# Attention and a feed-forward layer on one core: idle PE products at the start, norms spread over the last iterations, and the last down products in four banks

## The reference, cut to what matters

```python
x = x + _layernorm(_L0_attn_ref(_layernorm(x, axis=-1), L0_attn_Wq, L0_attn_Wk, L0_attn_Wv, L0_attn_Wo, ...))
x = x + _layernorm(_L0_ffn_ref(_layernorm(x, axis=-1), L0_ffn_w_gate, L0_ffn_w_up, L0_ffn_w_down), axis=-1)
...
maha = jnp.maximum(qn[..., None] + (E * E)[None] * kn[:, :, None, :] - 2.0 * E[None] * s, 0.0) / V[None]
logits = coef * jnp.log1p(maha / nu[None, :, None, None]) - 0.5 * DH_ * jnp.log(V)[None]
A = jax.nn.softmax(logits, axis=-1)
...
h = jax.nn.silu(gate) * up
return jnp.einsum('bsh,dh->bsd', h, wd)
```

## Time and profile before

| | |
|---|---|
| median of 3 runs | 1877.73 us (1877.56 to 1878.31) |
| profiled execution | 1878.49 us, span 1876.7 us |
| PE busy | 1792.1 us (95%) |
| DVE busy | 1628.9 us (87%) |
| ACT busy | 1580.4 us (84%) |
| POOL busy | 1469.7 us (78%) |
| mean granted clock of PE | 0.988 |

### The profile page before, as it was taken

How to read it: one execution, slowest core, us unless ns; L and a number is a source line. 1 busy time by engine, 2 the same in 40 slices (tenths; PEclk the granted TensorE clock), 3 DMA queues, 4 the chain that set the end, 5 groups by cost and what they waited for, 6 DMA issues and landing times.

```text
span 1876.7 us, 35392 instructions
## 1 busy us (share of the span) xinstructions
PE 1792.1 (95%) x10672; PEld 1476.5 (79%) x10672; DVE 1628.9 (87%) x3848; ACT 1580.4 (84%) x3259; POOL 1469.7 (78%) x1291
## 2 busy tenths in 40 slices
PE   4799999999999999999999999999999999988996
PEld 3577788878888888778888888788888888867886
DVE  7799989988988889888888999888988988895884
ACT  5798889898888889898988888988988888885563
POOL 5677888878888888888888888788888888862663
...
GB/s 187 114 68 46 85 46 68 46 102 46 63 52 90 64 49 44 45 124 46 68 46 99 32 63 52 82 89 49 46 42 91 46 46 46 68 13 12 46 47 44
DMA packets 61085, 117.77 MB, mean 63 GB/s; under 512 B 13489, under 2 KB 42929, under 8 KB 52705
## 3 DMA queue, kind: packets, MB, share of 16 engines
...
q10 hardware_dynamic: 384, 0.00, 0.0%
...
## 4 chain that ended last, share of the span: by engine, by line
PE 72%; DVE 10%; ACT 4%; issue 3%; POOL 1%; DVEq 0%; POOLq 0%; ACTq 0%
PE pa L759 15%; PE py L823 13%; PE ps L799 12%; PE po L834 10%; PE pp L789 8%; PE pp L811 6%; PE pa L770 4%; PE pa L778 2%; DVE lg L1603 2%; DVE stats L1630 1%; DVE rm L1472 1%; DVE acc L1652 1%; DVE tabs L1690 1%; DVE lg L1596 1%; POOL rstd L602 1%
## 5 line engine op out<-in xcount | busy, mean ns | idle before, releaser
L583 POOL TENSOR_TENSOR qk<-rm 64x512 f32<-64x512 f32 x504 | 697.2, 1383 | 93.2 <-PE ps L799 49.1
L593 POOL TENSOR_TENSOR ek<-tabs,kn 128x512 f32<-128x512 f32 (+3 forms) x512 | 463.8, 912 | 126.4 <-DVE lg L1596 99.4
L1603 DVE CUSTOM_DVE_ANT_0 lg<-lg,tabs,ncog 128x512 f32<-128x512 f32 (+3 forms) x512 | 446.7, 890 | 0.0
L759 PE MATMUL pa<-xt,wt 128*128 128x512 f32 x1488 | 421.9, 419 | 4.4 <-DVE rm L1478 2.7
L1472 DVE TENSOR_TENSOR rm<-pa,tabs 128x512 f32<-128x512 f32 x504 | 327.2, 677 | 74.1 <-POOL qk L583 66.1
L799 PE MATMUL ps<-qk 128*128 128x512 f32 (+3 forms) x1024 | 366.5, 442 | 7.8 <-DVE lg L1596 7.6
L823 PE MATMUL py<-pt,vt 128*128 128x128 f32 x2560 | 348.5, 275 | 0.1
L1596 DVE CUSTOM_DVE_ANT_0 lg<-ps,ek,qb 128x512 f32<-128x512 f32 (+3 forms) x512 | 279.3, 546 | 79.3 <-issue 61.1
L823 PEld LDWEIGHTS py<-pt,vt 128*128 128x128 f32 x2560 | 331.7, 192 | 16.2 <-issue 0.3
L759 PEld LDWEIGHTS pa<-xt,wt 128*128 128x128 f32 x1488 | 274.0, 191 | 56.9 <-issue 6.2
L1169 ACT ACTIVATE lg<-lg,qb 128x512 f32<-128x512 f32 (+3 forms) x512 | 273.0, 557 | 14.4 <-DVE lg L1596 10.4
...
## 6 DMA issues: line engine op xcount, KB each, us to landing
...
```

Source lines behind the costliest of these rows:

```text
L583: pool.tensor_tensor(qk[part * DH:(part + 1) * DH, z * HH + hh, :], rm[row, 2 * part, :], rm[row, 2 * part + 1, :], ALU.add if part else A ...
L593: pool.tensor_tensor(ek[:, n % 2, 0:w], tab(par, hh, E2_T, w), kn[:, hh, 0:w], ALU.mult).then_inc(ek_pool, 1)
L759: last = mm(pa[r][:, :], wproj(par, z, kt, a, r * P, (r + 1) * P), xbuf[x][:, kt, b, :], start=(n == 0), stop=(n == 3 * KT - 1))
L1603: dve.tensor_tensor_reduce(lg[:, hh, at(n)], lg[:, hh, at(n)], tab(par, hh, T3_T, w), ncog[:, par, 0, hh:hh + 1], 3e38, ALU.add, ALU.min, ...
```

## The change

*Preparation.* `keep_busy(n)` puts n products of the identity with the token numbers into PE's queue, plain f32, 512 columns, into the two `ps` banks; nobody reads them. Six stand ahead of `x_turn`, one between the two halves of the projections, two ahead of `first_norms_k`.

*Last iterations.* `left` is the number of iterations still to come. The first sequence's `first_norm(0)` moves into the iteration with `left` 3, its residual sum into `left` 2, its `second_norm(0)` into `left` 1, each on DVE between `decay(1,3)` and `distance(1,3)`; the powers on POOL move with them. In the last iteration all four distances of the second head are computed ahead of `add_output`, ACT takes `log(1,3)` with the other logarithms, `f_normal(0)` and `f_high(0)` come ahead of the exponentials, and PE takes `f_transposes(0)` and the first two `gate_up` earlier. The second sequence's norms are spread between `add_output`s.

*Tail.* The last sequence's down products go into four banks, a tile each: parts 0 to 4 of tiles 2 and 3, then of tiles 0 and 1, then part 5 of all. `f_last` is cut in two halves; of the last sequence ACT takes tiles 0 and 1 and DVE tiles 2 and 3 (`last_half`), and there are two stores. `third_norm` waits for two tiles at a time.

```diff
...
@@ -182,2 +182,7 @@
         po = bank("po")
+        last_banks = [py, po, pp[0], pp[1]]
+
+        def down_at(b, j):
+
+            return last_banks[j][:, 0:D] if b == B - 1 else (py, po)[j // 2][:, (j % 2) * D:(j % 2 + 1) * D]
 
...
@@ -530,6 +535,10 @@
                 f_load(b)
-            for b in range(B - 4, B):
+            for b in range(B - 4, B - 1):
                 f_store(b)
-            for s in range(2):
-                sp.wait_ge(f_out[s], 16 * (B // 2))
+            for k, half in enumerate((1, 0)):
+                sp.wait_ge(f_res, B + k)
+                sp.dma_start(out_d[B - 1].rearrange("(j p) n -> p j n", p=P)[:, 2 * half:2 * half + 2, :],
+                             f_outs[(B - 1) % 2][:, 2 * half:2 * half + 2, :]).then_inc(f_out[(B - 1) % 2], 16)
+            sp.wait_ge(f_out[0], 16 * (B // 2))
+            sp.wait_ge(f_out[1], 16 * (B // 2 + 1))
 
@@ -616,4 +625,6 @@
                     low_weights(pool, g, q)
-                if not nxt:
+                if it.left == 2:
                     f_pow(0, 0)
+                if not nxt:
+                    f_pow(1, 0)
                 if nxt:
@@ -627,4 +638,2 @@
                 decay_norm(c, 1, 2, it.par)
-                if not nxt:
-                    f_pow(1, 0)
                 if nxt:
@@ -642,4 +651,2 @@
                     x_rstd(it.own + 3)
-                if not nxt:
-                    f_pow(0, 1)
                 if nxt:
@@ -687,2 +694,3 @@
 
+            f_pow(0, 1)
             f_pow(1, 1)
@@ -889,2 +897,16 @@
 
+            def last_down():
+                b = B - 1
+                for tiles, parts in (((2, 3), range(FT - 1)), ((0, 1), range(FT - 1)), (range(NT), range(FT - 1, FT))):
+                    pe.wait_ge(f_hl, b * FT + parts[-1] + 1)
+                    for j in tiles:
+                        if parts[0] == 0 and j < 2:
+                            pe.wait_ge(f_ev, 2 * (b - 1) + j + 1)
+                        for r in parts:
+                            for a in range(2):
+                                last = mm(last_banks[j][:, 0:D], hpart(b, r, a)[:, j * P:(j + 1) * P], wdt[:, r, :],
+                                          start=(r == 0 and a == 0), stop=(r == FT - 1 and a == 1))
+                        if parts[0] and j % 2:
+                            last.then_inc(f_dn, 1)
+
             PERS = (8, 4, 2, 1)
...
@@ -994,2 +1019,8 @@
 
+            def keep_busy(n):
+
+                for k in range(n):
+                    mm(ps[k % 2][:, :], ident[:, :], tokens, start=True, stop=True)
+
+            keep_busy(6)
             x_turn(c0, 0, 0)
@@ -999,2 +1030,3 @@
             project(c0, 0, 0, 0, 0, 0, 0, 1)
+            keep_busy(1)
             pe.wait_ge(w_lo, 2 * KT)
@@ -1004,2 +1036,3 @@
             x_turn(c0, 1, 1)
+            keep_busy(2)
             first_norms_k()
...
@@ -1054,4 +1085,3 @@
                 gate_up(b, 5)
-            down(B - 1, 0)
-            down(B - 1, 1)
+            last_down()
 
@@ -1222,3 +1252,3 @@
 
-            def f_last(b):
+            def f_last(b, half):
                 act.wait_ge(f_move[2], b + 1)
@@ -1227,7 +1257,6 @@
                 q = 4 + b % 2
-                for j in range(NT):
-                    last = act.activation(f_tmp[:, j, :], (py, po)[j // 2][:, (j % 2) * D:(j % 2 + 1) * D], ACT.Identity,
+                for j in (2 * half, 2 * half + 1):
+                    last = act.activation(f_tmp[:, j, :], down_at(b, j), ACT.Identity,
                                           bias=f_shift[:, 6 + b % 2, j:j + 1], scale=f_rstd[:, q, j:j + 1])
-                    if j % 2 == 1:
-                        last.then_inc(f_ev, 1)
+                last.then_inc(f_ev, 1)
 
...
@@ -1387,2 +1419,4 @@
                 silu(b, 4)
+                if b == B - 1:
+                    f_last(b - 1, 0)
                 hidden_high(b, 4)
@@ -1390,4 +1424,6 @@
                 hidden_high(b, 5)
-                f_last(b - 1)
-            f_last(B - 1)
+                if b < B - 1:
+                    f_last(b - 1, 0)
+                f_last(b - 1, 1)
+            f_last(B - 1, 0)
 
@@ -1646,3 +1682,3 @@
 
-            def residual(b):
+            def residual_sum(b):
 
@@ -1653,2 +1689,4 @@
                 last.then_inc(f_sum, 1)
+
+            def second_norm(b):
                 dve.wait_ge(f_sum, b + 1)
@@ -1656,2 +1694,6 @@
 
+            def residual(b):
+                residual_sum(b)
+                second_norm(b)
+
             def second_move(b):
@@ -1660,4 +1702,7 @@
             def third_norm(b):
-                dve.wait_ge(f_dn, 2 * b + 2)
-                f_stat(2, b, lambda j: (py, po)[j // 2][:, (j % 2) * D:(j % 2 + 1) * D], EPS_LN / SCALE ** 2)
+                def source(j):
+                    if j % 2 == 0:
+                        dve.wait_ge(f_dn, 2 * b + j // 2 + 1)
+                    return down_at(b, j)
+                f_stat(2, b, source, EPS_LN / SCALE ** 2)
 
@@ -1678,2 +1723,20 @@
 
+            def last_half():
+                b = B - 1
+                dve.wait_ge(f_out[b % 2], (b // 2) * 16)
+                dve.wait_ge(f_move[2], b + 1)
+                for j in (2, 3):
+                    last = stt(f_outs[b % 2][:, j, :], down_at(b, j), f_rstd[:, 4 + b % 2, j:j + 1], acc[:, b, j, :],
+                               ALU.mult, ALU.add)
+                last.then_inc(f_sum, 1)
+                dve.wait_ge(f_sum, B + 1)
+                for j in (2, 3):
+                    last = ts(f_outs[b % 2][:, j, :], f_outs[b % 2][:, j, :], f_shift[:, 6 + b % 2, j:j + 1], None, ALU.add)
+                last.then_inc(f_res, 1)
+
+            def last_sum():
+                b = B - 1
+                dve.wait_ge(f_ev, 2 * b + 1)
+                tt(f_outs[b % 2][:, 0:2, :], f_tmp[:, 0:2, :], acc[:, b, 0:2, :], ALU.add).then_inc(f_res, 1)
+
             def split_low(b):
@@ -1712,4 +1775,3 @@
                 if not nxt:
-                    dve.wait_ge(acc_dve, 4 * (B * G - B + 1) + 4)
-                    first_norm(0)
+                    second_move(0)
                 if nxt:
@@ -1737,4 +1799,2 @@
                 logits(c, 0, 3, it.par)
-                if not nxt:
-                    residual(0)
                 decay(c, 1, 2, it.par)
@@ -1752,2 +1812,5 @@
                 distance(c, 1, 2, it.slot)
+                if not nxt:
+                    decay(c, 1, 3, it.par)
+                    distance(c, 1, 3, it.slot)
                 if old:
@@ -1759,5 +1822,6 @@
                     inverse(cp, 1)
-                if not nxt:
-                    second_move(0)
                 logits(c, 1, 1, it.par)
+                if not nxt:
+                    logits(c, 1, 2, it.par)
+                    split_low(0)
                 if nxt:
@@ -1767,5 +1831,13 @@
                     add_output(cp, it.b_before, it.over, 0, 1)
-                if not nxt:
-                    first_norm(1)
-                decay(c, 1, 3, it.par)
+                if nxt:
+                    decay(c, 1, 3, it.par)
+                else:
+                    logits(c, 1, 3, it.par)
+                if it.left == 3:
+                    dve.wait_ge(acc_dve, 4 * (B * G - B + 1) + 4)
+                    first_norm(0)
+                if it.left == 2:
+                    residual_sum(0)
+                if it.left == 1:
+                    second_norm(0)
                 if it.own is not None and it.own < 5:
...
@@ -1809,12 +1882,13 @@
             c = counts(dve, G * B - 1, PERS)
-            logits(c, 1, 3, 1)
+            first_norm(1)
             inverse(c, 0)
-            split_low(0)
-            residual(1)
+            residual_sum(1)
             add_output(c, B - 1, False, 0, 0)
+            second_norm(1)
             inverse(c, 1)
-            second_move(1)
             add_output(c, B - 1, False, 0, 1)
+            second_move(1)
             hidden(0, 0)
             add_output(c, B - 1, False, 1, 0)
+            hidden(0, 1)
             add_output(c, B - 1, False, 1, 1)
@@ -1823,3 +1897,2 @@
             dve.wait_ge(acc_dve, 4 * B * G + 4)
-            hidden(0, 1)
             hidden(0, 2)
@@ -1852,3 +1925,4 @@
             third_move(B - 1)
-            f_final(B - 1)
+            last_half()
+            last_sum()
 
```

33 lines of the change are left out of this document (19 added, 14 removed).

## The result

The changed kernel takes 1871.72 us (median of 9, 1870.08 to 1872.21), the kernel before, measured beside it, 1876.90 (9 runs, 1873.55 to 1878.39): ratio 0.9974, 95% interval 0.9963 to 0.9984. It is faster, by 5.2 us of medians, and by 6.8 from profiled run to profiled run (1878.49 to 1871.72, span 1876.7 to 1869.9). The forecast was 1863.9 with a range of 1859.5 to 1870.5: the direction was right, the gain 5.2 us of the 13.8 that were forecast, and the time 1.2 us outside the range.

A forecast was written before the change was run, and what follows sets the result against it. PE bounds steady attention; the hand-over to the feed-forward layer and the tail lose time to waits and low clock. Preparation 0, last iterations -9.1 (-9.6 with norms +0.5), tail -4.7: -13.8, giving 1863.9 us, range 1859.5 to 1870.5.

The forecast's parts named there:

- Preparation, 0: Start of the kernel: nine idle products speed up `project`, but the gain hides behind DVE's chain: 0, bounds +3 and -2.6.
- the forecast's signs: For the preparation: PE's first `project` passes in half the time, yet DVE's `x_low` at 13.7 as now.
- The cover by DVE: Preparation: DVE's own work sets when `x_low` starts, hiding a quick `project`; without that cover the gain would be 2.6 us.
- The moved norms, +0.5: Iterations 61 to 63: norms and residual sum on DVE at a place idle 1.07 us cost +0.5 us, bounds 0 and 6.8.
- The bound that stood beside it: Moved norms: upper bound of 6.8 us, if all their DVE time lay on PE's path.
- rival 2: Iterations 61 to 63: the moved norms are paid in full on PE's path, 6.8 us, time 1870; chance 0.05.
- The last iteration, -9.6: `exp(0,0)` to `gate_up(0,2)`: ACT work moved, table loads and low clock gone, 11.3 less 1.7 of new waits; bounds -5, -13.
- The hand-followed chain: Last iteration, followed instruction by instruction with trace durations: `gate_up(0,2)` at 1706.4, 9.6 less than 1716.03.
- The tail, -4.7: Last down products to end of span: earlier products -2.4, the rest from statistics, halved sums and store; bounds -2 and -6.5.
- The Trainium skill's rule on the store: Last store: a fixed cost of about 2.0 us makes a half store take 2.7, gaining 0.7 instead of 0.8.
- The base: Starting time: -13.8 taken from the median 1877.73 us, with stretches read from a profiled execution of 1878.49 us.

The follow-up runs named there:

- experiment 6: The nine idle products of the preparation taken out of the changed kernel, 1871.94 us, and put alone into the kernel before, 1876.12 us.
- early_load: The changed kernel with the residual-input loads of sequences 0 and 1 issued in iteration 57, not behind iteration 61's hidden-state load: 1869.13 us.
- spread: early_load with the first sequence's norms and residual sum cut into nine pieces at two idle places of DVE's order, iterations 58 to 62: 1864.55 us.
- experiment 7: The kernel before with the new tail, and norms and early loads as in spread, but the last iteration's old order on every engine: 1868.87 us.
- tail_alone: The kernel before with the new tail alone (banks, order of down products, half sums, half stores): 1870.70 us.
- idle_products_alone: The kernel before with the nine idle products of the preparation alone: 1876.12 us.

## Why the forecast was wrong, step by step

- **Preparation, 0.** Right as far as it can be measured (experiment 6), with some luck in the reason. In the changed kernel the first `x_low` starts at 13.73, where it started at 13.72. The idle products ended at 11.4, forecast 11.6. But `project` did not take half the time, as the forecast's signs had it: 4.41 us in place of 5.30, since the granted clock fell to 0.50 in it. The cover by DVE was tried with 0.9 us and not with 2.6.
- **The moved norms, +0.5: the step that failed.** They cost 6.8 (5.93 and 0.9). The prediction put it this way: "A norm makes that chain 0.9 us late and PE still arrives together with it: cost 0 to 0.1", and the sum "up to 1.8 late". Three things were wrong. First, PE does not arrive together with a chain that is 0.9 late. In the kernel before `distance(0,0)` ends at 1616.25 and the `scores(0,2)` that it releases starts at 1616.84, a margin of some 0.5 us. In the changed kernel, whose rows were 0.85 late already, it ends at 1618.00, 0.9 later than that, and PE waits for it:

```profile
1618.05 0.70 PE L807 MATMUL ps<-qk 128*128 128x256 f32 x2 [0.20 <-DVE lg L1632]
```

  PE's rows behind are 0.5 later than those ahead (`project` at 1618.40, 1617.08 before), and at 1629.88 the 128x128 `scores` wait 0.27 us more, again for DVE, which is 2.06 late there: 0.5 again, and iteration 60 takes 26.09 us in place of 25.10. Second, the length: a norm is 2.4 us there and the sum with its shift 3.4 in early_load, of which 1.07 fit. Third, the sum's load was never looked at: the move was costed by DVE's durations, without asking when its operand arrives. That is 2.6 us by early_load. The remainder, 4.3, is DVE's work beyond the idle places, of which the sum has 2.3; spread takes all of it away.
- The bound that stood beside it, 6.8 us "if every microsecond of 1.95 + 2.9 + 1.95 lay on PE's path", and rival 2 built on it (1870, chance 0.05), met the number, by another mechanism than it named: not all 6.8 of DVE's work was paid, but 4.3 of it and a transfer. Its chance was far too low for a term whose row showed 1.07 us of room for pieces of 1.95 to 2.9.
- **The last iteration, -9.6.** Measured -10.1. The hand-followed chain from `exp(0,0)` to `gate_up(0,2)` was 22.1 us, and the trace has 22.70 (1690.86 to 1713.56), against 31.3 before; `exp(0,0)` kept its place within 1.5 us (6.1 late in a chain that was 7.7 late). No stretch at 0.50 lies between 1680 and 1710, and the two table loads are gone. The terms were split wrongly, though: nearly all went to ACT's order and the clock, and 4 to 5 us belong to DVE's freed time (experiment 7). The 10.1 counts from the run that had 10.2 us at the low clock; from the 54.52 and 54.78 of tail_alone and idle_products_alone it would be 7.5 and 7.8.
- **The tail, -4.7.** Measured -4.3: down products begin 2.28 us behind the last `gate_up` in place of 3.84, and 15.70 us from there to the end were forecast as 15.4. By its terms: to the first statistics -2.7 (forecast -2.4), from there to the store -1.0 (-1.5), the store -0.6 (-0.8). With the clock at 1.00 all through the down products (tail_alone, spread) it is -5.9 in both, inside the stated -2 to -6.5. The 48 products take 6.0 us there; the prediction's 2 x 3.04 is 6.1, not 5.9.
- The Trainium skill's rule on the store (DMA: Bandwidth & Descriptors, the fixed cost) gave 2.7 us for a half. The last half is issued at 1867.1, 2.8 us ahead of the end: on that rule and trace agree. The halves land 2.2 to 2.3 us after their issues and the 512 KB store ahead of them 2.9, which leaves some 1.5 us that do not shrink with the size, less than the 2.0 of the Trainium skill.
- **The base.** The sum was made from a run at 1878.49. The median of 9 later is 1876.90, and the 10.2 us at the low clock in its hand-over, which the forecast counted as a fixed 4.2 to win, are 3.4 in two of four traces with that order of PE and ACT. Of a change that removes such a stretch, only its mean can be won.

With the failed term mended, by a kernel that hides the norms, the forecast's time is nearly met: spread takes 1864.55 where 1863.9 was predicted for the change. From the base measured beside it that is a gain of 12.2, where the sum, with the norms at 0, says 14.3.

What stays open: how much of tail_alone's 6.0 is the mean of clock stretches, for which one profile a kernel is too little, and for the same reason how the 10.1 of the last iteration divide. Why the load lands 5.9 us after its issue in one kernel and 7.4 in another was not followed either.
